# Attention preparation rebuilt: bfloat16 parts stored once in DRAM, the first stack loaded in two pieces, and the preparation re-ordered on every engine

## What is computed

```python
q, k, v = split_heads(x @ Wq), split_heads(x @ Wk), split_heads(x @ Wv)   # 16 heads of 8 features
attn = softmax(einsum('bhqd,bhkd->bhqk', q, k) * 128 ** -0.5)
attn = attn + bias[None]                       # bias gathered from rel_table by relative position
out = layernorm(einsum('bhqk,bhkd->bhqd', attn, v), eps=1e-3) * gamma + beta
x = layernorm(x + out)
h = einsum('btd,pd->btp', x, hasher_w)         # product-key experts: the 4 best of 32 keys
vals, idx = top_k(einsum('btp,np->btn', h, keys), 4); w = softmax(vals)
x = layernorm(x + scale * sum_k w_k * (silu(x @ values_down[idx_k]) @ values_up[idx_k]))
```

## Time and profile before

| | us |
|---|---|
| median of 3 runs (312.96 to 313.03) | 312.98 |
| the profiled execution | 312.77 |
| its span, first to last instruction | 311.0 |
| PE busy in it | 283.6 (91%) |
| DVE busy in it | 231.8 (75%) |
| first maximum on DVE | 21.57 |
| first scores of round 0 on PE | 41.40 |

### The profile page before, as it was taken

How to read it: one execution, slowest core, us unless ns; L and a number is a source line. 1 busy time by engine, 2 the same in 40 slices (tenths; PEclk the granted TensorE clock), 3 DMA queues, 4 the chain that set the end, 5 groups by cost and what they waited for, 6 DMA issues and landing times.

```text
span 311.0 us, 9808 instructions
## 1 busy us (share of the span) xinstructions
PE 283.6 (91%) x4087; PEld 131.2 (42%) x4087; DVE 231.8 (75%) x516; ACT 199.1 (64%) x392; POOL 125.8 (40%) x209
## 2 busy tenths in 40 slices
PE   4878988999998989999999999999999999889991
PEld 2545232333333333343455543434555433284390
DVE  4547788988889969987798699977986952167673
ACT  2575276777676767789865667898665689902500
POOL 8393511101102751127556312297563033943133
PEclk9999999999999999999999999999999999999997
DMA  6475597359432303000403020006000000100002
GB/s 171 103 235 175 144 322 122 80 207 308 179 99 57 81 4 78 6 2 17 140 4 78 4 78 5 3 8 184 4 2 6 2 5 1 36 4 2 0 6 62
DMA packets 28265, 23.48 MB, mean 76 GB/s; under 512 B 6542, under 2 KB 26686, under 8 KB 28222
## 3 DMA queue, kind: packets, MB, share of 16 engines
q1 hardware_dynamic: 27950, 22.73, 25.9%
q10 hardware_dynamic: 272, 0.13, 0.1%
HBM read 12.18 MB, written 10.52 MB: 73 GB/s over the span
## 4 chain that ended last, share of the span: by engine, by line
PE 62%; DVE 15%; POOL 8%; ACT 7%; issue 4%; DMA 3%; SPq 1%; POOLq 0%; DVEq 0%
PE sm_ps L1139 13%; PE st_ps L1139 11%; PE ov_ps L1189 11%; DVE neg_max L838 9%; PE si_ps L1139 6%; PE mi_ps L1139 5%; ACT probs L713 3%; PE mi_ps L1195 2%; PE st_ps L1412 2%; POOL rstd L466 2%; PE sm_ps L1150 2%; DVE stats L877 2%; ACT w_rows L624 1%; DMA k_stack<-stack_dram 1%; PE si_ps L1213 1%
## 5 line engine op out<-in xcount | busy, mean ns | idle before, releaser
L838 DVE TENSOR_REDUCE neg_max<-sm_ps 128x1 f32<-128x512 f32 x256 | 166.0, 685 | 37.1 <-PE sm_ps L1139 30.9
L713 ACT ACTIVATE probs<-st_ps 128x512 f32<-128x512 f32 x256 | 138.3, 613 | 41.7 <-PE st_ps L1139 41.7
L1139 PE MATMUL sm_ps<-k_stack,q_stack 96*32 96x512 bf16 x928 | 91.6, 383 | 4.5 <-DVE neg_max L838 3.9
L1139 PE MATMUL st_ps<-q_stack,k_stack 128*32 128x512 bf16 x1024 | 89.0, 380 | 1.3 <-ACT bias_v L624 0.7
L1189 PE MATMUL ov_ps<-probs,v_cur 128*32 128x512 f32 x512 | 66.5, 592 | 0.0
L1139 PEld LDWEIGHTS sm_ps<-k_stack,q_stack 96*32 96x32 bf16 x928 | 24.7, 94 | 64.6 <-DVE neg_max L838 52.7
L480 POOL TENSOR_TENSOR hid<-hid,w_rows 128x512 f32<-128x512 f32 x26 | 32.9, 1281 | 36.1 <-ACT w_rows L624 36.0
L1139 PEld LDWEIGHTS st_ps<-q_stack,k_stack 128*32 128x32 bf16 x1024 | 27.5, 96 | 34.8 <-ACT probs L713 16.0
L901 DVE SCALAR_TENSOR_TENSOR hid<-tanh_sb,mi_ps 128x512 f32<-128x512 f32 x24 | 16.3, 680 | 12.0 <-ACT tanh_sb L750 12.0
L1139 PE MATMUL mi_ps<-x_t,down_sb 128*32 128x512 f32 x192 | 25.0, 592 | 0.0
L1139 PE MATMUL si_ps<-up_sb,hid 128*32 128x128 f32 x768 | 24.0, 272 | 0.0
(11 more groups left out here) (166 smaller groups left out, 297.3 us busy)
## 6 DMA issues: line engine op xcount, KB each, us to landing
stack_dram<-parts SPq DMA_DIRECT2D x18, 384.0 KB, 4.5
q_stack<-stack_dram SPq DMA_DIRECT2D x16, 288.0 KB
k_stack<-stack_dram SPq DMA_DIRECT2D x16, 288.0 KB
stack_dram<-parts SPq DMA_DIRECT2D x6, 288.0 KB, 4.4
x_sb<-L_attn_x SPq DMA_DIRECT2D x4, 256.0 KB, 3.9
out<-y_out SPq DMA_DIRECT2D x3, 256.0 KB, 2.3
stack_dram<-parts SPq DMA_DIRECT2D x6, 96.0 KB, 2.1
down_sb<-L_ffn_values_down SPq DMA_DIRECT2D x1, 512.0 KB, 9.0
```

Of the source, the lines that this page charges most:

```text
L713: nc.scalar.activation(probs[:, u % 2, j, :], st_ps[:, score_bank(u * J + j), :], ACT.Exp, scale=SCORE_SCALE).then_inc(probs_ready, 1)
L838: nc.vector.tensor_reduce(neg_max[:, g % 2, col:col + 1], sm_ps[:, c % 2, :], AX.X, ALU.max, negate=True).then_inc(max_ready, 1)
L1139: i = nc.tensor.matmul(dst[n * TILE:(n + 1) * TILE], weights[:, n * TILE:(n + 1) * TILE], moving, **flags)
```

## The change

Preparation is rewritten, and steps 0 to 3 of round 0 take some of its work; behind them the streams of PE, ACT, DVE and POOL are as before, and SP's differ in the form of writes and loads only.

- **DRAM holds each part once.** `parts_dram` has 24 rows of 16 x 512 elements for each of q and k. A part is written once (32 KB for four heads, 96 KB for twelve, 128 KB for a batch; a third of before), and as soon as it is made: the high parts of q and k first, then the middle, then the low. The repeats are made by the load: its source has a step of zero over 3, inside the 24 rows for q, outside them for k. A row of a slice is then 4 KB in one piece, before four pieces of 1 KB.
- **The first slice comes in two pieces** of two heads, each q then k (`load_heads`, semaphores `first_pair` and `stack_loaded0`); the relative table's window and the expert keys are loaded between the writes of the first set and this load.
- **Weights** are loaded by ACT's queue at its start; x of all batches follows directly on SP's.
- **PE** turns x of batches 0 and 1 first, then multiplies by Wq and Wk of batch 0, turns batches 2 and 3, and goes through the rest without a maximum between. The turned x lies in `hid` for all four batches. The first maximum stands behind the v of batch 3. Batch 3's k and q products are put off to behind maximum 18 and ahead of maximum 24. Each bias product is followed by one maximum, and maxima 9 to 18 are made in four 32-column pieces (`tiled`).
- **DVE** copies v (before ACT did). **ACT** takes the last batch's parts in the bias copies and in round 0: two copies for k behind the first `bias_keep`, two for q in step 0, two middle parts in step 3. **POOL** makes that batch's low parts in round 0, and its spread constants ahead of the first `split_shift`.

```diff
-        stack_dram = nc.dram_tensor("stack_dram", [B, 2, H, D * PARTS * PARTS, S], BF16, kind="Internal").ap()
+        parts_dram = nc.dram_tensor("parts_dram", [B, 2, PARTS * D, H, S], BF16, kind="Internal").ap()
...
+        def x_t(b):
+            return hid[:, b, :]
...
+            def load_heads(t, heads, loaded):
+                for a, stack in enumerate((q_stack, k_stack)):
+                    rows = [[H * S, PARTS * D], [0, PARTS]] if a == 0 else [[0, PARTS], [H * S, PARTS * D]]
+                    src = bass.AP(parts_dram.tensor, (t * 2 + a) * PARTS * D * H * S + heads.start * S,
+                                  rows + [[1, (heads.stop - heads.start) * S]])
+                    sp.dma_start(stack[0:TERMS, heads, :], src).then_inc(loaded, 16)
             def load_slice(t, g):
                 if not is0(t):
                     sp.wait_ge(scores_ready, (t - 1) * (J * U) + J * C * (g + 1))
                     apart(sp)
-                for a, stack in enumerate((q_stack, k_stack)):
-                    src = stack_dram[t, a, g * J:(g + 1) * J]
-                    sp.dma_start(stack[0:TERMS, g * J:(g + 1) * J, :], src.rearrange("h r s -> r h s")) \
-                      .then_inc(stack_loaded[g], 16)
+                load_heads(t, slice(g * J, (g + 1) * J), stack_loaded[g])
...
-                sp.dma_start(x_sb[:, b], x[b].rearrange("(c p) e -> p c e", p=P)).then_inc(x_loaded[b], 16)
-                if b == 0:
-                    for dst, src in ((wq_sb, w_q), (wk_sb, w_k), (wv_sb, w_v)):
-                        sp.dma_start(dst[:], src).then_inc(proj_loaded, 16)
+                load_x(b)
...
             def write_parts(b, heads, written):
-                for a in range(2):
-                    sp.wait_ge(*((first_split, a + 1) if b == 0 else (low_made, split_count(b, a))))
-                    rows = stack_dram[b, a, heads].rearrange("h (d i j) s -> (h d) i j s", i=PARTS, j=PARTS)
-                    for n in range(PARTS):
-                        dst = rows[:, :, n, :] if a == 0 else rows[:, n, :, :]
-                        sp.dma_start(dst, parts[heads.start * D:heads.stop * D, b, a]).then_inc(written, 16)
+                for i in range(PARTS):
+                    for a in range(2):
+                        if b:
+                            sp.wait_ge(low_made, split_count(b, a))
+                        else:
+                            sp.wait_ge(*((high_made, a + 1), (first_mid, a + 1), (first_split, a + 1))[i])
+                        rows = parts_dram[b, a, :, heads].rearrange("(i d) h s -> i h d s" if a == 0 else
+                                                                   "(d i) h s -> i h d s", i=PARTS)
+                        sp.dma_start(rows[i], parts[heads.start * D:heads.stop * D, b, a, i]).then_inc(written, 16)
             write_parts(0, slice(0, J), first_written)
+            load_tables()
             sp.wait_ge(first_written, 2 * PARTS * 16)
             sp.wait_ge(stack_set, 1)
             sp.wait_ge(rows_cleared, 1)
-            load_slice(0, 0)
+            load_heads(0, slice(0, J // 2), first_pair)
+            load_heads(0, slice(J // 2, J), stack_loaded[0])
             write_parts(0, slice(J, H), parts_written[0])
...
+            add_beta(0)
+            add_beta(1)
+            low_parts(1)
+            low_parts(2)
+            pool.wait_ge(v_copied, B)
             for g in range(G):
                 fetch_values(0, g)
-            for a in range(2):
-                pool.wait_ge(last_copied, a + 1)
-                nc.gpsimd.tensor_sub(resid[:, 1, a], resid[:, 1, a], parts[:, B - 1, a, 0, :]).then_inc(last_resid, 1)
-            split_shift(0, 0)
-            low_parts(B - 1)
+            add_beta(2)
...
+            add_beta(3)
+            split_shift(0, 0)
+            for n, a in enumerate((1, 0)):
+                pool.wait_ge(last_copied, n + 1)
+                nc.gpsimd.tensor_sub(resid[:, 1, a], resid[:, 1, a], parts[:, B - 1, a, 0, :]).then_inc(last_resid, 1)
...
+                if is0(t):
+                    low_parts(B - 1)
...
+            for dst, src, loaded in ((wq_sb, w_q, proj_loaded[0]), (wk_sb, w_k, proj_loaded[1]), (wv_sb, w_v, proj_loaded[2])):
+                nc.scalar.dma_start(dst[:], src).then_inc(loaded, 16)
+            x_copy(0)
+            x_copy(1)
+            high_parts(0)
+            middle_parts(0)
...
+            bias_copy(CG)
+            bias_copy(G - 1)
+            shift_copy(0, 0)
+            def last_parts(a):
+                act.wait_ge(qk_made, 2 * B - a)
+                copy(parts[:, B - 1, a, 0, :], qk_bank(B - 1, a)).then_inc(high_made, 1)
+                act.wait_ge(low_made, split_count(1, a))
+                copy(resid[:, 1, a], qk_bank(B - 1, a)).then_inc(last_copied, 1)
+            bias_keep(CG)
+            last_parts(1)
...
+                    if u == 0 and is0(t):
+                        last_parts(0)
+                    if u == 3 and is0(t):
+                        middle_parts(B - 1)
...
+            resids(0)
+            for a in range(2):
+                dve.wait_ge(first_mid, a + 1)
+                nc.vector.tensor_sub(parts[:, 0, a, 2, :], resid[:, 0, a], parts[:, 0, a, 1, :]).then_inc(first_split, 1)
+            v_copy(0)
+            resids(1)
+            v_copy(1)
+            resids(2)
+            v_copy(2)
+            v_copy(3)
...
+                if is0(t) and pos == 0 and c == 0:
+                    pe.wait_ge(first_pair, 32)
+                elif pos % J == (J // 2 if is0(t) and pos < J else 0) and c == 0:
...
+            early_maxima(EARLY, J * C + 2, tiled)
+            pe.wait_ge(table_copied, 3)
+            make_qk(B - 1, 1)
+            pe.wait_ge(consts_made, 8)
+            pe.wait_ge(shift_split, 1)
+            turn(mi_bf[:, 0:P], shift_parts[:].rearrange("p i n -> p (i n)"), ident_bf[:]).then_inc(misc_ready, 1)
+            early_maxima(1, EARLY)
...
+            pe.wait_ge(misc_done, 1)
+            make_qk(B - 1, 0)
```

More of the change, by code:

```diff
@@ new lines, in turn_x, with make_qk @@
+                for c in range(C):
+                    i = nc.tensor.transpose(turned_bank(b)[:, c * P:(c + 1) * P], x_sb[:, b, c, :], ident[:])
+                i.then_inc(x_turned, 1)
+            def make_qk(b, a):
+                pe.wait_ge(xt_copied, b + 1)
+                if b >= 2:
+                    pe.wait_ge(high_made, 2 * (b - 2) + a + 1)
+                    pe.wait_ge(resid_made, 2 * (b - 2) + a + 1)
+                nc.tensor.matmul(qk_bank(b, a), (wq_sb, wk_sb)[a][:], x_t(b), start=True, stop=True).then_inc(qk_made, 1)
@@ L1290, in _, with early_maxima @@
             early = [divmod(k, C) for k in range(EARLY)]
-            def early_maxima(n, most=J * C + 2):
+            def early_maxima(n, most=J * C + 2, product=whole):
                 for _ in range(n):
                     if early and EARLY - len(early) < most:
-                        maximum_scores(0, *early.pop(0), product=whole)
-            for b in range(B):
-                prep(b)
-            early_maxima(2)
-            pe.wait_ge(rel_loaded, 16)
-            pe.wait_ge(prep_copied, 4 * (B - 1) + 4)
@@ L1318, in _, with bias_turn, bias_product @@
-            pe.wait_ge(table_copied, 3)
+                        maximum_scores(0, *early.pop(0), product=product)
+            def bias_turn(g):
+                pe.wait_ge(bias_copied, g - CG + 1)
+                pe.wait_ge(v_copied, B) if g == CG else pe.wait_ge(bias_kept, g - CG + 1)
+                for c in range(C):
+                    i = turn(bias_banks(g)[1][:, c * P:(c + 1) * P], bias_t[:, g % 2, c * P:(c + 1) * P], ident[:])
+                i.then_inc(bias_turned, 1)
+            def bias_product(g, kc):
+                n = constant_from((g + 1) * J - 1) + 1
+                for j in range(J):
+                    h = g * J + j
+                    window = bass.AP(rel_t, S - 1 - HPB * h + (P // H) * kc, [[pitch, P], [HPB, n], [-1, HPB]])
+                    i = nc.tensor.matmul(bias_banks(g)[0][j * TILE:(j + 1) * TILE, 0:n * HPB],
+                                         v_all[:, kc, h].rearrange("p b d -> p (b d)"), window,
+                                         start=(kc == 0), stop=(kc == C - 1))
+                if kc == C - 1:
+                    i.then_inc(bias_mm, 1)
@@ new lines, in _ @@
+            pe.wait_ge(consts_made, 2)
+            turn_x(0)
+            turn_x(1)
+            pe.wait_ge(proj_loaded[0], 16)
+            make_qk(0, 0)
+            pe.wait_ge(proj_loaded[1], 16)
+            make_qk(0, 1)
+            turn_x(2)
+            turn_x(3)
+            pe.wait_ge(proj_loaded[2], 16)
+            make_v(0)
+            make_qk(1, 0)
+            make_qk(1, 1)
+            make_v(1)
+            make_qk(2, 0)
+            make_qk(2, 1)
+            make_v(2)
+            pe.wait_ge(high_made, 4)
@@ new lines, in _ @@
+            pe.wait_ge(resid_made, 4)
+            pe.wait_ge(rel_loaded, 16)
```

(15 more changed lines are left out.)

191 lines of the change are left out of this document (70 added, 121 removed).

## The result

| | before | after |
|---|---|---|
| median of four runs on one chip, us | 313.0 | 321.9 (320.9 to 322.4) |
| ratio after / before, 95% interval | | 1.028 (1.025 to 1.031) |
| span of the profiled execution | 311.0 | 320.3 |
| first maximum on DVE | 21.57 | 21.54 |
| first scores of round 0 on PE | 41.40 | 45.52 |

The prediction was 312.8, with a range up to 317.0. The changed kernel lies outside it, on the slow side. The last two rows of the table part the loss of 9.3 us in the span: 4.1 lie ahead of round 0, 5.2 behind its start.

The account below looks back on a forecast made before the run. PE, busy 91% of the span, bounds from round 0 on, so only the preparation's chain of waits could move: -1.3 us there, +0.5 in round 0, +0.6 in round 1, sum -0.2, forecast 312.8 us, range 308.5 to 317.0.

Parts of the forecast that it names:

- The opening and first writes: In the preparation: 0.5 us of delay from turning batch 1 first; last write issued at 12.65, landed at 14.6.
- Three engines, at 26 GB/s each: k's loads, outermost count 3, run on three engines; a k slice of 98 kB an engine takes 3.8 us.
- slower engines: Rival for k's loads: three engines at a slower pace, 319.5 us at 20 GB/s an engine; chance 0.25.
- The loads are spread: Rival: k flows over 12 or 16 engines, round 0 starts at 37.2, 309.1 us in all; chance 0.27.
- First maximum at 19.5: On DVE in the preparation: k's first piece lands at 19.1, first maximum at 19.5, 2.1 us earlier than before.
- its four terms: Maxima between the first one and the split: 4 at 0.66, 4 at 0.8, 4 at 0.73, 4 at 0.94, summed as 12.4 us.
- The new wait: Before round 0: shift load lands behind k's slices at 40.3; round 0 starts 1.1 us earlier, not 4.2.
- That sum: Second set's writes on the three engines: 2.2 us with overhead behind a piece ending at 21.1, landing at 23.8.
- Slice 1 lands just ahead of maximum 17: In the preparation: slice 1 lands at 30.5, just ahead of maximum 17 at 31.
- Round 0's copies, +0.5: ACT's added copies in steps 0 and 3 of round 0 push back an exponential: +0.5 us (0 to 1.2).
- Round 1's slice, +0.6: Slice with head 8, issued at 88.48, lands at 95.1 against use at 94.71: +0.6 us (0 to 1).
- The writes of a third of the size ... nothing waited for them: Smaller writes free the DMA engines, but nothing waited for them outside the preparation, so no gain was counted.

Follow-up runs that it names:

- experiment 1: The changed kernel with k's load as three transfers of 24 partitions each in place of one with an outermost repeat of 3: 310.92 us, ratio to before 0.994.
- experiment 8: The changed kernel with k's loads of rounds 0 and on in three transfers of 24 partitions, the preparation's k loads left on three engines: 317.33 us.
- experiment 5: The changed kernel with only the first shift load moved on SP from behind slices 2 and 3 to between slices 1 and 2: 321.52 us.
- experiment 2: The changed kernel with parts stored three times and loaded as 72 distinct rows, as in the kernel before: 310.07 us, ratio 0.990.
- experiment 7: The changed kernel with four more fp32 products on PE ahead of the wait for the first piece, so PE does not stand still: 321.82 us.
- experiment 9: The changed kernel with k loaded in three transfers and batch 0's parts written for all 16 heads in the first six writes: 308.17 us, ratio 0.985.
- experiment 4: The changed kernel with the first shift load issued by ACT behind its copy instead of standing in SP's queue: 321.91 us.

## Why the prediction was wrong

- **The opening and first writes: right.** Last issue at 12.37 and landed by 14.5 (forecast 12.65 and 14.6).
- **Three engines, at 26 GB/s each: right**, both of them (share 0.19 to 0.20, 76 to 80 GB/s), and experiments 1 and 8 show that they are the cause. The rival "slower engines" came in by half: beside other loads they were slower. Slice 1's q was in by 30.3 and its k by 35.9, so 98 kB took an engine some 5.5 us, 18 GB/s; slices 2 and 3, with hardly a load beside them, went at 26. Its 319.5 us is nearer to the result than the forecast's 312.8. "The loads are spread" did not happen; made to happen in experiment 1, it gave 310.9 where that rival said 309.1.
- **First maximum at 19.5: wrong, by 2.0 us.** PE was there early (17.8, forecast 18.7). k's first piece landed at 20.99 and not at 19.1, 5.5 us from its issue in place of 3.8. I had used the pace of engines that are alone; that the two q loads, which flow on the same three engines and beside them, took it away is my explanation, and no run took them out. The split followed at 34.54 (forecast 31.9; its four terms make 12.5, not 12.4, and 13.0 passed).
- **The new wait: the step that failed.** The mechanism is as forecast, the shift load behind k's slices on the same three engines, and its size is off by 5.2 us: it landed at 45.48, forecast 40.3. Of these, 2.8 are there when the second set of writes has landed (26.64, forecast 23.8). The last of them landed 4.8 us behind its issue, against 2.3 in experiment 1: k's second piece held the three engines until 24.57, forecast 21.1. (That sum did not close either: 21.1 and 2.2 are 23.3.) 2.6 are slice 1: 9.3 us from the writes' landing in place of 6.7. Slices 2 and 3 took 4.6 and 4.8 us, as forecast (4.75). That slice 1 was slow because of the slices behind it is shown by experiment 5: with nothing behind it, 6.8 us from k's issue to landing, 8.5 with them. That it was their q loads, which flowed meanwhile, is the likely part of it, not tried by itself.
- **"Slice 1 lands just ahead of maximum 17": wrong for the same reason.** PE waited 2.2 us, and the turn of the shift rows waited with it: issued at 38.03, forecast 33.8.
- **Round 0's copies, +0.5: wrong.** They cost nothing (experiment 2). Round 0 lost 0.9 us all the same, with the halved clock after PE had waited, which was in no term (no loss in experiment 1 without a halved stretch, 1.9 in experiment 7 with a longer one).
- **Round 1's slice, +0.6: mis-sized.** It was 3.5 (2.8 the wait, 0.7 behind it at the halved clock), and 0.4 each in rounds 2 and 3, for which the text had "4 us or more to spare". The slice took 9.0 us from issue to use instead of 6.65: the issues are 0.85 and 0.73 us, and the next slice's q load flows beside it, two things that the 6.65 did not hold; what each cost was not tried.
- **"The writes of a third of the size ... nothing waited for them": right** (experiment 2), until the second set is given up (experiment 9).

Added up: the forecast had -0.2 us, the span grew by 9.3. Of these 9.5 us, 5.2 are the new wait, 3.7 the slices of later batches, 0.6 round 0.

In one line: the prediction had the right bottleneck and costed it as if each transfer had it to itself.

The Trainium skill, page "DMA: Bandwidth & Descriptors", section "Rules for kernel authors", warns of a leading zero-stride repeat that confines a load to at most as many engines as there are copies. Experiment 1 puts a number to that here, 11 us.

## What to carry to other kernels

Before an access pattern is made shorter, ask what its outermost count becomes: here 3 in place of 72 meant three DMA engines in place of twelve, and the 6.3 MB saved did not make up for it. A resource shared by a long load and a small urgent one must be costed as a queue, from the first transfer on it to the last, with everything that flows beside it, and with the issues that stand behind it on SP. When an edit that frees the start of a stage moves the total by nothing, look for the next wait of the same kind further on before the theory is dropped: in experiment 5 it was one group of heads later.

## What the runs showed of the hardware that I had not expected

- **Loads from DRAM in rows of 4 KB: 26 GB/s an engine with three busy, 14 to 17 with twelve** (experiment 1). In all, twelve engines moved 172 to 207 GB/s, no more than the 198 to 233 of the kernel before in rows of 1 KB. The prediction had its 26 from a stretch of writes (3 KB rows), where sixteen engines kept it, so the number of busy engines alone does not set the pace. The median packet of 4 KB took 159 ns in the changed kernel from 27 to 46 us, and one in ten 287 ns or more; in experiment 1, 229 ns was the median from 27 to 33. What holds the loads back was not found.
- **An issue's time on SP doesn't follow its number of packets.** A load of 72 rows of 4 KB takes 0.70 to 0.85 us to issue; the load of before, 288 rows of 1 KB, mostly took 0.29 to 0.43 (up to 1.25 in later rounds); 24 rows of 4 KB take 0.35, or 0.53 where they come first of three. Why was not tried.
- **One issue on SP can take as long as a transfer**: `up_sb` from 2.9 us (experiment 1) over 5.7 (experiment 2) and 6.6 (experiment 5) to 8.0 (experiment 4). What it waits for was not isolated.
- **The granted clock falls to 1.2 GHz after PE has stood still**, behind each of the changed kernel's three long waits (3.3, 4.0 and 2.6 us), and costs about 0.9 us where PE is the bound afterwards. It stayed up through a wait of 2.2 us (33.7 to 36.0). With PE kept busy through the wait the clock stayed up (experiment 7).
